# Top-2 expert stage: three tiles in flight, and one PSUM bank per tile for transposed rows and down products

## The reference

```python
gate_logits = xf @ gate_w.T
weights, indices = jax.lax.top_k(gate_logits, TOP_K)       # TOP_K = 2, 8 experts
weights = jax.nn.softmax(weights, axis=-1)
combine = zeros((N, E)).at[arange(N)[:, None], indices].add(weights)
for e in range(E):
    h = jax.nn.silu(xf @ w1[e].T) * (xf @ w3[e].T)         # 128 -> 384
    y = h @ w2[e].T                                        # 384 -> 128
    out = out + combine[:, e:e + 1] * y
```

## Time and profile before

| what | value |
|---|---|
| median of three runs | 795.96 us (795.4 to 797.33) |
| the profiled execution | 797.43 us, its span 795.6 us |
| mean granted TensorE clock | 0.79 |
| the changed stage, first gather to last scatter | 545.70 to 771.00 us of the span |
| PE, PEld, DVE, ACT, POOL busy over the span | 65, 52, 60, 33, 47% |

### The profile page before, as it was taken

The page is one execution under the profiler, slowest core; times in us unless marked ns, Lnnn a source line. Parts: engine busy times, 40 slices in busy tenths (PEclk is TensorE's granted clock), DMA queues, the critical chain, the costliest instruction groups (busy, mean ns, idle before and its releaser), DMA issues.

```text
span 795.6 us, 12900 instructions
## 1 busy us (share of the span) xinstructions
PE 520.7 (65%) x4447; PEld 413.3 (52%) x4447; DVE 473.6 (60%) x1178; ACT 264.1 (33%) x627; POOL 372.4 (47%) x345
## 2 busy tenths in 40 slices
PE   4999722223484665069999978415978887878850
PEld 2455521111153544037777758314867877878840
DVE  5365568898711112298999997695535344444427
ACT  1122133322522121037777774121323223223225
POOL 2000000000168887347888862065676666676740
PEclk9999855555877787558999996555999889898995
DMA  9700145000035453720000002450111111111129
GB/s 302 304 26 28 50 84 149 0 0 0 9 97 138 97 142 34 171 54 2 2 4 2 3 2 80 94 144 23 38 44 41 44 43 42 40 46 39 47 65 285
DMA packets 65245, 56.04 MB, mean 70 GB/s; under 512 B 10176, under 2 KB 59200, under 8 KB 65056
## 3 DMA queue, kind: packets, MB, share of 16 engines
q1 hardware_dynamic: 49904, 38.45, 16.9%
q0 software_dynamic: 10688, 14.04, 8.4%
q10 hardware_dynamic: 4592, 2.75, 1.3%
HBM read 35.37 MB, written 19.86 MB: 69 GB/s over the span
## 4 chain that ended last, share of the span: by engine, by line
PE 31%; POOL 20%; DVE 18%; issue 17%; DMA 6%; another core or an unknown queue 4%; ACT 3%; DVEq 0%; SPq 0%; POOLq 0%; ACTq 0%
PE psum L1351 7%; POOL arena L556 6%; PE psum L1608 6%; PE psum L1625 5%; PE psum L1330 4%; PE psum L1614 4%; DVE arena_b L738 3%; POOL scratch L502 3%; POOL v_x L546 2%; DMA arena<-normed,gather_i 2%; POOL results L591 2%; POOL y_odd L512 2%; POOL x_tok L539 2%; POOL y_even L512 1%
## 5 line engine op out<-in xcount | busy, mean ns | idle before, releaser
L502 POOL DMA_INDIRECT scratch<-table,idx x32 | 33.8, 1055 | 218.2 <-DVE idx_w L852 208.7
L591 POOL DMA_INDIRECT results<-arena,dest_i x71 | 74.5, 1049 | 51.3 <-ACT arena L1307 33.6
L1108 DVE TENSOR_TENSOR arena<-arena,psum 128x384 f32<-128x384 f32 x71 | 39.2, 553 | 88.9 <-remote 31.7
L583 POOL DMA_INDIRECT arena<-normed,gather_i x71 | 78.2, 1101 | 26.9 <-issue 20.7
L1330 PE MATMUL psum<-cst,arena 128*128 128x128 f32 x327 | 58.1, 293 | 43.8 <-issue 17.7
L1301 ACT ACTIVATE arena<-psum 128x384 f32<-128x384 f32 x71 | 35.2, 495 | 124.0 <-PE psum L1608 85.0
L556 POOL TENSOR_TENSOR arena<-arena,peak 128x1024 f32<-128x1024 f32 x32 | 60.9, 1904 | 30.4 <-DVE peak L940 30.4
L1625 PE MATMUL psum<-arena_b,arena 128*128 128x128 f32 x426 | 67.9, 301 | 0.3 <-issue 0.2
L1330 PEld LDWEIGHTS psum<-cst,arena 128*128 128x128 f32 x327 | 41.8, 150 | 49.3 <-issue 41.2
L1608 PE MATMUL psum<-arena 128*128 128x128 f32 x426 | 66.2, 297 | 0.0
L1614 PE MATMUL psum<-arena 128*128 128x128 f32 x426 | 65.5, 292 | 0.5 <-issue 0.3
(11 more groups left out here) (236 smaller groups left out, 1116.7 us busy)
## 6 DMA issues: line engine op xcount, KB each, us to landing
arena<-in_w_down_dram SPq DMA_DIRECT2D x8, 768.0 KB
w_sb<-in_w_dram SPq DMA_DIRECT2D x3, 1536.0 KB, 13.9
x_tok<-in_x_dram SPq DMA_DIRECT2D x4, 512.0 KB, 7.8
y_odd<-zeros SPq DMA_DIRECT2D x4, 512.0 KB
table<-xn SPq DMA_DIRECT2D x8, 256.0 KB, 2.3
y_even<-x_tok SPq DMA_DIRECT2D x16, 128.0 KB
extra<-y_odd ACTq DMA_DIRECT2D x4, 512.0 KB, 11.5
x_tok<-y_even SPq DMA_DIRECT2D x4, 512.0 KB, 10.5
```

The source lines that it names most:

```text
L502: nc.gpsimd.indirect_dma_start(out=rows_b[:, e // 4 % 4, e % 4, :], out_offset=None, in_=table[:, :], in_offset=bass.IndirectOffsetOnAxis( ...
L583: nc.gpsimd.indirect_dma_start(out=rows_d[:, t % ROWS_D, :], out_offset=None, in_=normed[:, :], in_offset=bass.IndirectOffsetOnAxis(ap=gat ...
L591: nc.gpsimd.indirect_dma_start(out=results[:, :], out_offset=bass.IndirectOffsetOnAxis(ap=dest_i[:, t:t + 1], axis=0), in_=y_d[:, t % 4, : ...
L1108: nc.vector.tensor_tensor(act_d[:, b, :], silu_d[:, b, :], psum[:, 3 + b, 0:FF_D], ALU.mult).then_inc(e_act, 1)
```

## The change

The stage's loops get one more tile between the up products and the down product. The up products have three banks each (1 to 3 and 4 to 6). Banks 0 and 7 are left, and bank 7*(t%2) holds both the down product of tile t (columns 0 to 127) and the transposed rows of tile t+4 (columns 128 to 255), which ACT takes with one copy into `yx_d`. Only the first four tiles' rows have a copy of their own. Row buffers go from 8 to 6, result buffers from 4 to 6, gathers run six tiles ahead instead of five, and the weight buffers change places in SBUF.

```diff
-ROWS_D = 8
+ROWS_D = 6
+OUT_D = 6
+X_AHEAD = 4
...
 POOL, gather(t) and the lead
-                if t >= ROWS_D:
+                if ROWS_D <= t < ROWS_D + X_AHEAD:
                     pool.wait_ge(e_tr, t - ROWS_D + 1)
+                if t >= ROWS_D + X_AHEAD:
+                    pool.wait_ge(e_yp, t - ROWS_D - X_AHEAD + 1)
...
-            AHEAD = 5
+            AHEAD = 6
...
 DVE
             for t in range(3):
                 tile_weights(t)
+            for t in range(2):
                 down_weights(t)
             for t in range(RUN_D):
                 product(t)
                 if t + 3 < RUN_D:
                     tile_weights(t + 3)
-                    down_weights(t + 3)
+                if t + 2 < RUN_D:
+                    down_weights(t + 2)
...
 ACT
             def silu(t):
                 act.wait_ge(e_h1, t + 1)
-                if t > 1:
-                    act.wait_ge(e_act, t - 1)
+                if t > 2:
+                    act.wait_ge(e_act, t - 2)
...
             def evac_y(t):
                 act.wait_ge(e_yp, t + 1)
-                if t >= 4:
-                    act.wait_ge(e_st[t % 4], 16 * (t // 4))
-                nc.scalar.copy(y_d[:, t % 4, :], psum[:, 5 + t % 2, 0:P]).then_inc(e_y, 1)
+                if t >= OUT_D:
+                    act.wait_ge(e_st[t % OUT_D], 16 * (t // OUT_D))
+                n = 2 * P if t + X_AHEAD < RUN_D else P
+                nc.scalar.copy(yx_d[:, t % OUT_D].rearrange("p k c -> p (k c)")[:, 0:n],
+                               psum[:, 7 * (t % 2), 0:n]).then_inc(e_y, 1)
...
+            for t in range(X_AHEAD):
+                first_rows(t)
+            for t in range(2):
+                silu(t)
             for t in range(RUN_D):
-                if t + 1 < RUN_D:
-                    silu(t + 1)
-                if t > 0:
-                    evac_y(t - 1)
-                if t + 3 < RUN_D:
-                    rows_t(t + 3)
-            evac_y(RUN_D - 1)
+                if t + 2 < RUN_D:
+                    silu(t + 2)
+                evac_y(t)
...
 PE
             def rows_t(t):
                 pe.wait_ge(e_ld[t % ROWS_D], 16 * (t // ROWS_D + 1))
-                if t > 0:
-                    pe.wait_ge(e_xt, t)
-                transpose(psum[:, 0, 0:P], rows_d[:, t % ROWS_D, :]).then_inc(e_tr, 1)
+                if t == 1:
+                    pe.wait_ge(e_w, 1)
+                if 2 <= t < X_AHEAD + 2:
+                    pe.wait_ge(e_xt, t - 1)
+                if t >= X_AHEAD + 2:
+                    pe.wait_ge(e_y, t - X_AHEAD - 1)
+                ins = transpose(psum[:, 7 * (t % 2), P:2 * P], rows_d[:, t % ROWS_D, :])
+                if t < X_AHEAD:
+                    ins.then_inc(e_tr, 1)
...
             def up(t):
-                b = t % 2
+                b = t % 3
                 pe.wait_ge(e_w, t + 1)
-                pe.wait_ge(e_xt, t + 1)
-                if t > 1:
-                    pe.wait_ge(e_silu, t - 1)
+                if t < X_AHEAD:
+                    pe.wait_ge(e_xt, t + 1)
+                else:
+                    pe.wait_ge(e_y, t - X_AHEAD + 1)
+                if t > 2:
+                    pe.wait_ge(e_silu, t - 2)
...
-            for t in range(3):
+            for t in range(X_AHEAD):
                 rows_t(t)
-            up(0)
+            for t in range(2):
+                up(t)
             for t in range(RUN_D):
-                if t + 1 < RUN_D:
-                    up(t + 1)
-                if t + 3 < RUN_D:
-                    rows_t(t + 3)
+                if t + 2 < RUN_D:
+                    up(t + 2)
+                if t + X_AHEAD < RUN_D:
+                    rows_t(t + X_AHEAD)
                 down(t)
```

More of the change, by code:

```diff
@@ L281, in metaformer @@
         rows_d, at = shared(arena, 0, [P, ROWS_D, P])
[L282 to L288, removed]
+        silu_d, at = shared(arena, at, [P, 3, FF_D])
+        act_d, at = shared(arena, at, [P, 3, FF_D])
+        yx_d, at = shared(arena, at, [P, OUT_D, 2, P])
+        w2_t, at = shared(arena, at, [P, 4, CHUNKS_D, P])
+        w13_t, _ = shared(arena_b, 0, [P, 3, 2, FF_D])
         back1 = extra
@@ L395, in metaformer @@
         e_ld = [sem(f"e_ld{i}") for i in range(ROWS_D)]
-        e_st = [sem(f"e_st{i}") for i in range(4)]
+        e_st = [sem(f"e_st{i}") for i in range(OUT_D)]
         f_back = [sem(f"f_back{i}") for i in range(BLOCKS)]
@@ L477, in _ @@
             results_v = results[0:PAIRS, :].rearrange("(k t p) c -> k p t c", k=2, p=P)
-            for b in range(4):
-                sp.wait_ge(e_st[b], 16 * len(range(b, RUN_D, 4)))
+            for b in range(OUT_D):
+                sp.wait_ge(e_st[b], 16 * len(range(b, RUN_D, OUT_D)))
             for n in range(BLOCKS):
@@ L593, in scatter @@
                     out_offset=bass.IndirectOffsetOnAxis(ap=dest_i[:, t:t + 1], axis=0),
[L594 to L597 removed]
+                    in_=yx_d[:, t % OUT_D, 0, :], in_offset=None, bounds_check=last_result,
+                    oob_is_err=True).then_inc(e_st[t % OUT_D], 16)
+            AHEAD = 6
             for t in range(AHEAD):
@@ L1291, in _, with first_rows @@
                                      scale=C("partition")).then_inc(d_ohp, 1)
[L1293 removed]
+            def first_rows(t):
                 act.wait_ge(e_tr, t + 1)
[L1295 removed]
+                nc.scalar.copy(yx_d[:, (t - X_AHEAD) % OUT_D, 1, :], psum[:, 7 * (t % 2), P:2 * P]).then_inc(e_xt, 1)
             def silu(t):
                 act.wait_ge(e_h1, t + 1)
[L1299 to L1301 removed]
+                if t > 2:
+                    act.wait_ge(e_act, t - 2)
+                nc.scalar.activation(silu_d[:, t % 3, :], psum[:, 1 + t % 3, 0:FF_D], ACT.Silu).then_inc(e_silu, 1)
             def evac_y(t):
                 act.wait_ge(e_yp, t + 1)
[L1305 to L1319 removed]
+                if t >= OUT_D:
[7 more added lines that the diff above has]
+                silu(t)
+            for t in range(RUN_D):
+                if t + 2 < RUN_D:
+                    silu(t + 2)
+                evac_y(t)
             for n in range(BLOCKS):
@@ L1624, in down @@
                 for k in range(CHUNKS_D):
-                    ins = nc.tensor.matmul(psum[:, 5 + b, 0:P], act_d[:, b, P * k:P * (k + 1)],
+                    ins = nc.tensor.matmul(psum[:, 7 * (t % 2), 0:P], act_d[:, t % 3, P * k:P * (k + 1)],
                                            w2_t[:, t % 4, k, :], start=k == 0, stop=k == CHUNKS_D - 1)
                 ins.then_inc(e_yp, 1)
-            for t in range(3):
+            for t in range(X_AHEAD):
                 rows_t(t)
-            up(0)
+            for t in range(2):
+                up(t)
             for t in range(RUN_D):
-                if t + 1 < RUN_D:
-                    up(t + 1)
-                if t + 3 < RUN_D:
-                    rows_t(t + 3)
+                if t + 2 < RUN_D:
+                    up(t + 2)
+                if t + X_AHEAD < RUN_D:
+                    rows_t(t + X_AHEAD)
                 down(t)
```

20 lines of the change are left out of this document (9 added, 11 removed).

## The result

| | before | after |
|---|---|---|
| median (20 runs each, side by side) | 797.74 us (794.74 to 801.32) | 793.05 us (789.24 to 797.52) |
| ratio, 95% interval | 1 | 0.9948 [0.993, 0.9967] |
| profiled execution, its span | 797.43, 795.6 us | 792.93, 791.1 us |
| first gather, first scatter, end of last scatter | 545.70, 559.18, 771.00 | 548.26, 562.92, 766.15 |
| the stage, first gather to last scatter | 225.3 us | 217.9 us |

The forecast was no change that can be told. The kernel got faster by 4.7 us in the median. Timed again beside the kernel before in experiment 9, it was faster by 2.4 us.

The account below looks back on a forecast made before the run. POOL's indirect DMAs were taken as the base load, with only its waits to win. Terms -0.35 + 2.8 - 3.5 + 2 = +1.0 us gave 798.4 us profiled, 797.0 against the median; own range 793 to 801, whole range 781 to 806.

Parts of the forecast that it names:

- What bounds the stage: POOL's indirect DMAs are the base load, 2.70 us a tile; only what its waits add, 29.4 us, can be won.
- Its signs: Expected in the changed trace: 15 to 20 waits, sum 25 to 35 us, copy near 0.38 us, silus up to 4 us late.
- Rival 2: Lateness is made by the order of work and three tiles cover it: all 29.4 us of waits go, 766 to 769; chance 0.11.
- Start: Up to the first scatter: it comes 1.0 us late, one gather turn of 1.35 us less behind it; sum -0.35 us.
- The stops: POOL's waits for ACT's copy: 17.5 instead of 16, +2.8 us; each some 0.2 us shorter, -3.5 us.
- the count of units: PE's groups of six matmuls: each result needs one more, as many issued at a stop; cycles 4.0 tiles instead of 4.4.
- The turn: POOL's time for one indirect DMA: all 142 stay, so the base of 1.35 us a turn stays.
- Clock: PE's half clock of 1.2 GHz: part of the slow time moves behind POOL's stop, +2 us (-4 to +8).

Follow-up runs that it names:

- experiment 9: The changed kernel as it is, timed again beside the kernel before: 0.9976 of the kernel before, 798.37 us.
- 7: The changed kernel with results stored by SP's plain DMAs, not to their places, POOL issuing gathers alone: 0.9196 of the kernel before, 735.65 us.
- 13: The changed kernel with results stored by SP's plain DMAs and every gather issued twice, the second unused: 0.9931 of the kernel before, 795.13 us.
- 14: The changed kernel with rows loaded by SP's plain DMAs, unsorted, and scatters still POOL's: 0.9207 of the kernel before, 737.21 us.
- Experiment 3: The changed kernel with PE's down product ahead of the up product and ACT's copy ahead of the silu: 0.9962 of the kernel before.
- experiment 4: The kernel before with gathers seven tiles ahead instead of five: 0.9999 of the kernel before.
- experiment 1: The kernel before with ACT's copy of the down product ahead of the next tile's silu: 0.9985 of the kernel before.
- experiment 8: The changed kernel with a memset of 128x640 on POOL behind every third scatter: 0.999 of the kernel before.
- 2: The changed kernel with two PSUM banks for each up product instead of three: 0.9949 of the kernel before.
- 10: The changed kernel with ACT's copy of tile t behind the silu of tile t+3: 1.009 of the kernel before, 807.38 us.
- 5: The kernel before with ACT's copy ahead of the silu and gathers seven tiles ahead: 0.9976 of the kernel before.
- 12: The changed kernel with the shared bank taken in two ACT copies of 128x128, product first: 0.9967 of the kernel before.
- 6: The kernel before with ACT's copy first, gathers seven tiles ahead and transposed rows alternating between banks 0 and 7: 0.9971 of the kernel before.

## Why the prediction was wrong

- **What bounds the stage: right.** POOL's 142 turns are the base, and the stops are the rest. Experiments 7, 13 and 14 show what the prediction only argued, that readers see PE's products late while POOL issues indirect DMAs without pause. Its signs were there too: 19 waits with 29.8 us (21 with 34.3 in experiment 9), a copy of 0.37 us, restarts one microsecond behind POOL's stop, and PE's idle time (37.8 us) in front of the first up product. Rival 2, full decoupling, is excluded: the lateness doesn't come from the order, since the same order keeps the beat as soon as POOL has pauses.
- **Start: right.** -0.35 said; +1.1 - 1.35 = -0.25 measured, and +0.3 - 1.35 = -1.05 in experiment 9.
- **The stops: +2.8 - 3.5 = -0.7 said; -3.7 in one execution and +1.6 in the other.** Their mean is -1.0, so no error is shown here. The means of 1.84 and 1.43 us are no fair pair, because short waits count in them. Of waits over 1.1 us the kernel before has 15 of 1.90 us, the changed kernel 14 of 1.64 and 17 of 1.72 in its two executions: 0.26 and 0.18 us shorter, where the prediction said 0.2. Their number moved both ways, so neither its 17.5 nor the count of units behind it is tested by two traces. Experiment 3, which that count favoured, gained nothing, as the wait moved to a silu that the count leaves out.
- **The turn: the step that failed.** "All 142 indirect DMAs stay: the base of 1.35 us a turn stays." The number of DMAs stayed and the turn did not. It fell to 1.325 us in both traces of the changed kernel, worth -3.4 and -3.5 us where the prediction had nothing. The traces around them fit: 1.340 in the kernel before with a longer lead (experiment 4), 1.326 in the kernel before with ACT's copy first (experiment 1), and 1.30 to 1.33 in all others that compute everything but experiment 8, whose memsets add to it. The gathers' mean fell from the earlier trace rows's 1101 ns to 1073. About half or more of the term is that fewer indirect DMAs start just behind one of DVE's weight copies; what the rest is stays open. The prediction took 1.35 us as a constant of POOL, though the earlier trace rows had a gather of 1.41 us among others of about 1.04. With one trace of the kernel before, the size of the term is less sure than its sign.
- **Clock: not borne out.** +2 said. In the stretch behind the first scatter the granted clock was 0.91 before, 0.95 after and 0.93 in experiment 9. With levels at 1.0 and 0.5 that is an estimate of 2 x 0.09 x 211.8 = 38 us at 1.2 GHz before, and of 20 and 29 us after. So PE was slow for less time and not for more. What this gave back was not measured by itself.

With the turn's term and without the clock's, the prediction's own sum would be -0.35 - 0.7 - 3.4 = -4.5 us, where it said +1.0. Measured are -7.4 and -3.0 us for the stage in two executions, and -4.7 and -2.4 us in the medians. That this falls so close is in part luck, as the stops' term alone moved by 5 us between executions.

What of the change does it? Shown is that the third bank adds nothing that can be told (2), and that the changed kernel loses when ACT's shared copy goes behind the next silu (10). Neither the copy's place alone (1: -0.15%), nor the lead alone (4: 0), nor both (5: -0.24%) reaches -0.5% for sure, and the one wide copy (12) is no gain. But 5 and 6, which have no third tile in flight, stand where the changed kernel stood when it was timed again (-0.24%). So the deeper order itself is not shown to be worth anything, and how the gain is shared stays open: the intervals of +-0.0025 don't part the pieces.

## What to carry to other kernels

When a consumer starts microseconds behind the recorded end of a matmul with nothing queued before it, ask before deepening the pipeline whether POOL is issuing indirect DMAs back to back. One of the two kinds replaced by plain DMAs was worth 8% here, in kernels that leave out part of the computation; a way that keeps it was not tried. A pause bought with POOL's own time gave back what it cost. Where such stops remain, their length follows from what stands ahead of the awaited copy on its engine: on average 1.8 to 1.9 us with a silu there (before, 4, 10), 1.4 to 1.8 without, counting those over 1.1 us. Yet shorter stops alone gave no gain that can be told (1), since more of them came. Treat the base of a sum as a term too: here its 2% a turn was as large as all that was argued about. Read a term off two executions before it carries a conclusion. Count buffers last: a third PSUM bank that no wait shows short is worth nothing.

## What the runs showed of the hardware

- In the expert stage readers saw PE's products over 4 us late while POOL issued two indirect DMAs a tile without pause (silus up to 4.09 us in the kernel before, ACT's copies up to 4.31 in the changed one, silus up to 3.25 in experiment 13), and at most 0.04 us late with one a tile (7 and 14). At the stops of over 1.3 us behind the first scatter, ACT's first start came 0.79 to 1.25 us after POOL fell idle before the change (14 stops) and 0.83 to 1.18 us after it (13 stops), and others followed in a burst. The stage takes (766.15 - 548.26)/71 = 3.07 us a tile with 142 such DMAs, and PE's beat is 2.12 us with 71, whichever 71 they are.
- An indirect DMA of 128 rows holds POOL for 1.03 to 1.04 us and 0.30 us pass before the next. By these rows, 142 of them would need some 190 us; that is an estimate of the stage without lateness, which no run shows.
- An indirect DMA that begins 0.05 to 0.3 us behind the start of one of DVE's copies of 128x768 or 128x384 f32 ends some 0.9 us behind that copy's end, so it takes up to 1.41 us instead of 1.04 (585.94, 626.83 and 631.07).
- ACT's copy of 128x256 from PSUM takes 0.37 us, where a 128x128 took 0.265 to 0.270.
